# Value products of two tiles in one stretch, row sums of a head pair in one group, a third score bank

## What is computed

```
x_n = group_norm(x, 32 groups)                        # per image
qkv = einsum('bnc,oc->bno', x_n, qkv_w)               # 3 x 192 outputs
attn = softmax(einsum('bhnd,bhmd->bhnm', q, k) * 32 ** -0.5)
out = einsum('bhnm,bhmd->bhnd', attn, v)              # heads side by side: 192 channels
y = x + einsum('bnc,oc->bno', out, proj_w) + proj_b
```

## Time and profile before

| | |
|---|---|
| median of 3 runs | 1676.67 us |
| the profiled execution | 1676.28 us, its span 1674.5 us, granted clock 0.982 |
| TensorE busy | 1556.8 us (93%) |
| GpSimd busy | 1321.8 us (79%) |
| ScalarE busy | 1232.9 us (74%) |
| VectorE busy | 1188.9 us (71%) |
| value products | 3072 records, 409.8 us busy |
| row-sum products | 1152 records, 154.3 us busy |

### The profile page before, as it was taken

The page is one execution under the profiler, slowest core; times in us unless marked ns, Lnnn a source line. Parts: engine busy times, 40 slices in busy tenths (PEclk is TensorE's granted clock), DMA queues, the critical chain, the costliest instruction groups (busy, mean ns, idle before and its releaser), DMA issues.

```text
span 1674.5 us, 24581 instructions
## 1 busy us (share of the span) xinstructions
PE 1556.8 (93%) x8800; PEld 488.0 (29%) x8800; DVE 1188.9 (71%) x2022; ACT 1232.9 (74%) x2001; POOL 1321.8 (79%) x645
## 2 busy tenths in 40 slices
PE   3389999999999999999999999999999999999982
PEld 1123233232323333232332323232332323233220
DVE  3387878777787877777787777778787777777710
ACT  2138787887869787886968788796978778686770
POOL 3019888888978888888888888897888888788891
PEclk9979999999999999999999999999999999999995
DMA  2304042341515134152504325151513414141112
GB/s 71 57 26 83 15 88 47 75 86 52 103 38 103 27 85 76 52 108 52 95 25 94 57 68 93 52 103 38 98 34 77 83 52 83 52 71 33 46 34 68
DMA packets 86106, 108.87 MB, mean 65 GB/s; under 512 B 38240, under 2 KB 50912, under 8 KB 85984
## 3 DMA queue, kind: packets, MB, share of 16 engines
q1 hardware_dynamic: 85984, 107.30, 30.8%
HBM read 42.98 MB, written 13.15 MB: 34 GB/s over the span
## 4 chain that ended last, share of the span: by engine, by line
PE 80%; ACT 10%; issue 2%; DMA 1%; DVE 1%; SPq 0%; POOL 0%; POOLq 0%; ACTq 0%; DVEq 0%
PE heads_ps L550 21%; PE scores_ps L535 19%; PE max_ps L469 19%; PE sums_ps L567 7%; ACT probs L690 6%; PE extra_ps L518 2%; PE extra_ps L522 2%; PE extra_ps L519 2%; PE extra_ps L520 2%; PE extra_ps L523 2%; ACT heads_sb L653 1%; ACT xhat_b L642 1%; ACT x_res L620 1%; DMA inv_sb<-inv_rows 1%; PE extra_ps L498 0%
## 5 line engine op out<-in xcount | busy, mean ns | idle before, releaser
L844 DVE TENSOR_REDUCE half_max<-max_ps 128x1 f32<-128x512 f32 x1536 | 1005.2, 685 | 336.0 <-PE max_ps L469 321.8
L690 ACT ACTIVATE probs<-scores_ps,exp_scale 128x512 f32<-128x512 f32 x1536 | 994.1, 689 | 310.4 <-PE scores_ps L535 304.5
L743 POOL TENSOR_TENSOR prob_pairs<-probs 128x1024 f32<-128x1024 f32 x384 | 898.6, 2361 | 205.1 <-ACT probs L690 204.2
L469 PE MATMUL max_ps<-k_stack,q_stack 96*128 96x512 f16 x1536 | 593.5, 388 | 22.5 <-DVE half_max L844 13.5
L535 PE MATMUL scores_ps<-q_stack,k_stack 98*128 98x512 f16 x1536 | 586.4, 383 | 24.4 <-ACT probs L690 18.2
L550 PE MATMUL heads_ps<-probs,v_sb 128*32 128x512 f32 x3072 | 409.8, 606 | 0.1
L469 PEld LDWEIGHTS max_ps<-k_stack,q_stack 96*128 96x128 f16 x1536 | 149.7, 98 | 555.5 <-issue 429.6
L749 POOL TENSOR_TENSOR prob_pairs<-prob_pairs 128x1024 f32<-128x1024 f32 x96 | 224.3, 2358 | 0.0
L535 PEld LDWEIGHTS scores_ps<-q_stack,k_stack 98*128 98x128 f16 x1536 | 149.5, 98 | 237.3 <-ACT probs L690 171.3
L567 PE MATMUL sums_ps<-prob_pairs,ones 128*32 128x512 f32 x1152 | 154.3, 608 | 3.2 <-POOL prob_pairs L743 3.2
L550 PEld LDWEIGHTS heads_ps<-probs,v_sb 128*32 128x32 f32 x3072 | 60.5, 108 | 131.7 <-issue 129.9
(11 more groups left out here) (82 smaller groups left out, 940.0 us busy)
## 6 DMA issues: line engine op xcount, KB each, us to landing
q_stack<-qk_hi SPq DMA_DIRECT2D x96, 128.0 KB, 4.2
k_stack<-qk_hi SPq DMA_DIRECT2D x96, 128.0 KB, 5.6
inv_sb<-inv_rows SPq DMA_DIRECT2D x48, 256.0 KB
x_res<-x SPq DMA_DIRECT2D x16, 768.0 KB, 5.5
out<-x_res SPq DMA_DIRECT2D x16, 768.0 KB, 4.6
x_sb<-x SPq DMA_DIRECT2D x16, 512.0 KB, 7.4
x_sb<-x SPq DMA_DIRECT2D x32, 256.0 KB, 8.7
q_stack<-qk_lo SPq DMA_DIRECT2D x48, 128.0 KB, 4.1
```

The source lines that it names most:

```text
L469: pe.matmul(max_ps[:, bank, :], q_stack[0:STACK, par, h, P * tile:P * (tile + 1)], k_stack[0:STACK, par, h, HALF * half:HALF * (half + 1)] ...
L690: nc.scalar.activation(probs[:, a, s % RING, HALF * half:HALF * (half + 1)], scores_ps[:, u_bank(s, u), :], ACT.Exp, scale=exp_scale[:, 0: ...
L743: nc.gpsimd.tensor_tensor(prob_pairs[:, a, q, :], probs[:, a, (s - 1) % RING, :], probs[:, a, s % RING, :], ALU.add).then_inc(pairs_added, 1)
L844: nc.vector.tensor_reduce(half_max[:, a, tile, half:half + 1], max_ps[:, bank, :], AX_X, ALU.max).then_inc(max_read[bank], 1)
```

## The change

The value products of two tiles stand together, in even slots, after unit 2 (`VALUES_UNIT`); odd slots have none. The three row-sum quads of a head pair are one small product of the kind `sums`, in slots 10, 18 and 2, in `extra_ps`: twelve products in a row, right behind the value products of the slot. ScalarE copies them at the start of the next slot (`take`), and `copy_sums` and the semaphores `sums_done` and `sums_taken` go. The bank `sums_ps` becomes a third score bank. The head copy comes after unit 3 instead of 2. The later steps of the sums' way come one slot earlier (`SUMS_SPREAD` to `DIVIDED`), the moves of head pairs 1 and 2 to attn (`MOVED`) one slot earlier too, and three small products change places: qk 16 to 15, projection 17 and 18 to 16 and 17.

```
-SCORE_BANKS = 2
+SCORE_BANKS = 3
...
-QK_SLOTS = (12, 16, 19)
+QK_SLOTS = (12, 15, 19)
-PROJ_SLOTS = (17, 18, 20, 22)
+PROJ_SLOTS = (16, 17, 20, 22)
+SUMS_SLOTS = {10: 0, 18: 1, 2: 2}
...
-SUMS_TAKEN = TILES + 4
-SUMS_SPREAD = TILES + 5
-INVERTED = TILES + 6
-INV_SPREAD = TILES + 7
-INV_GATHERED = TILES + 8
-DIVIDED = TILES + 11
-MOVED = (23, 22, 22)
+SUMS_SPREAD = TILES + 4
+INVERTED = TILES + 5
+INV_SPREAD = TILES + 6
+INV_GATHERED = TILES + 7
+DIVIDED = TILES + 10
+MOVED = (23, 21, 21)
-COUNT_UNIT, HEADS_UNIT, SUMS_UNIT = 3, 2, 3
+VALUES_UNIT, HEADS_UNIT = 2, 3
...
     (TensorE, fill)
+                elif kind == "sums" and part == 0:
+                    pe.wait_ge(pairs_added, READY[-1] * (PAIRS * st.summed(i) + i + 1))
+                    for q in range(QUAD_AT, PAIRS_A_HEAD):
+                        for half in range(HALVES):
+                            for a in range(2):
+                                at = D * (2 * half + a)
+                                last = pe.matmul(extra_ps[at:at + D, :], ones[:, 0:D],
+                                                 prob_pairs[:, a, q, HALF * half:HALF * (half + 1)],
+                                                 start=(q == QUAD_AT), stop=(q == PAIRS_A_HEAD - 1))
...
     (TensorE, step)
-                        if u == 1:
-                            if s == 0 and st.tail:
-                                weigh(st.b - 1, 1 - st.parity, SLOTS - 1)
-                            elif s > 0 and st.attend:
-                                weigh(st.b, st.parity, s - 1)
+                        if u == VALUES_UNIT and s % PAIR == 0:
+                            for tile in range(s - PAIR, s):
+                                if s == 0 and st.tail:
+                                    weigh(st.b - 1, 1 - st.parity, SLOTS + tile)
+                                elif s > 0 and st.attend:
+                                    weigh(st.b, st.parity, tile)
                         if u >= 2 and st.extra(s) is not None:
                             fill(st, s, u - 2)
-                        if u == COUNT_UNIT:
-                            for j, par, q in st.due(s, PAIR_COUNTED, PAIR):
-                                count(j, q)
...
     (ScalarE, take)
+                elif kind == "sums":
+                    k = PAIRS * st.summed(i) + i
+                    if due(k):
+                        act.wait_ge(sums_spread_out, MOVE * k)
+                    nc.scalar.copy(sums_sb[:, :], extra_ps[:, :]).then_inc(extra_freed, 1)
...
     (GpSimd, pair add)
-                            if a == 0 and q >= QUAD_AT and due(k):
-                                pool.wait_ge(sums_done, COUNTED[-1] * (k - 1) + COUNTED[q])
+                            if a == 0 and q == QUAD_AT and due(k):
+                                pool.wait_ge(extra_filled, st.ordinal(s - 1) + 1)
```

More of the change, by code:

```diff
@@ L71 @@
 V_SLOTS = (7, 8, 11, 14)
-QK_SLOTS = (12, 16, 19)
+QK_SLOTS = (12, 15, 19)
 QK_LATE_SLOTS = (3, 4, 6)
-PROJ_SLOTS = (17, 18, 20, 22)
-EXTRA_SLOTS = (*SHIFT_SLOTS, *V_SLOTS, *QK_SLOTS, *QK_LATE_SLOTS, *PROJ_SLOTS)
+PROJ_SLOTS = (16, 17, 20, 22)
+SUMS_SLOTS = {10: 0, 18: 1, 2: 2}
+EXTRA_SLOTS = (*SHIFT_SLOTS, *V_SLOTS, *QK_SLOTS, *QK_LATE_SLOTS, *PROJ_SLOTS, *SUMS_SLOTS)
 assert len(set(EXTRA_SLOTS)) == len(EXTRA_SLOTS)
@@ L82 @@
 PAIR = 2
-PAIR_COUNTED = PAIR + 3
 PAIRS_A_HEAD = TILES // PAIR
@@ L90 @@
 READY = (2, 6, 8, 10)
-COUNTED = (0, 1, 2, 3)
 HEADS_TAKEN = TILES
-SUMS_TAKEN = TILES + 4
-SUMS_SPREAD = TILES + 5
-INVERTED = TILES + 6
-INV_SPREAD = TILES + 7
-INV_GATHERED = TILES + 8
-DIVIDED = TILES + 11
-MOVED = (23, 22, 22)
-COUNT_UNIT, HEADS_UNIT, SUMS_UNIT = 3, 2, 3
+SUMS_SPREAD = TILES + 4
[5 more added lines that the diff above has]
+VALUES_UNIT, HEADS_UNIT = 2, 3
 STATS = 4
@@ L143, in extra @@
             return "proj", PROJ_SLOTS.index(s)
+        if s in SUMS_SLOTS and (self.tail if SUMS_SLOTS[s] == PAIRS - 1 else self.attend):
+            return "sums", SUMS_SLOTS[s]
         return None
@@ L154, in shifted, with summed @@
         return (self.b + 1, 1 - self.parity) if pair == 0 else (self.b, self.parity)
+    def summed(self, pair):
+        return self.b - 1 if pair == PAIRS - 1 else self.b
     def made(self, i):
@@ L214, in group_norm_attention @@
         heads_ps = psum("heads_ps", [P, HALF])
-        sums_ps = psum("sums_ps", [P, HALF])
         q_stack = sb("q_stack", [P, 2, HEADS, N], F16)
@@ L306, in group_norm_attention @@
         heads_done = sem("heads_done")
-        sums_done = sem("sums_done")
         heads_taken = sem("heads_taken")
-        sums_taken = sem("sums_taken")
         sums_spread_out = sem("sums_spread_out")
@@ L398, in step @@
                         k = PAIRS * j + p
-                        sp.wait_ge(sums_taken, k + 1)
+                        sp.wait_ge(extra_freed, st.ordinal(s - 2) + 1)
                         sp.dma_start(sums_spread[:, :], sums_sb[0:P:D, :]
@@ L554, in weigh @@
                 last.then_inc(heads_done, 1)
[L556 to L570, removed]
             pe.wait_ge(setup, SETUP)
@@ L600, in take @@
                 kind, i = s > 0 and st.extra(s - 1) or (None, 0)
-                if kind in ("qk", "v"):
+                if kind in ("qk", "v", "sums"):
                     g = st.ordinal(s - 1)
@@ L653, in copy_heads @@
                     nc.scalar.copy(heads_sb[:, (par + p) % 2, :], heads_ps[:, :]).then_inc(heads_taken, 1)
-            def copy_sums(st, s):
-                for j, par, p in st.due(s, SUMS_TAKEN, TILES):
-                    k = PAIRS * j + p
-                    act.wait_ge(sums_done, COUNTED[-1] * (k + 1))
-                    if due(k):
-                        act.wait_ge(sums_spread_out, MOVE * k)
-                    nc.scalar.copy(sums_sb[:, :], sums_ps[:, :]).then_inc(sums_taken, 1)
             def between(st, s, u):
@@ L671, in between @@
                     copy_heads(st, s)
-                if u == SUMS_UNIT:
-                    copy_sums(st, s)
                 if st.tail and (s, u) in BIAS_AT:
```

## The result

The changed kernel takes 1704.04 us (median of 4 runs, 1703.77 to 1704.85) against 1676.43 us of the kernel before beside it (4 runs, 1675.66 to 1676.68): ratio 1.0166, 95% interval 1.0149 to 1.0184. It is 27.6 us slower. The profiled execution took 1704.04 us with a span of 1702.3 us, to set beside 1676.28 and 1674.5.

What follows compares the result with a forecast made beforehand. Each slot was taken to end by TensorE's work or a 3.28 us loop through ScalarE; 24.9 for middle batches, 1.3 first, 0 last, 0.8 end made +27.0 on 1676.28, median 0.4 above: 1704 us, range 1673 to 1728.

Steps and rivals of the forecast that it cites:

- case A: Whole kernel: the doubled stretch starves VectorE and ScalarE, 1704 us, own range 1687 to 1722; chance 0.67.
- middle: 14 middle batches, each 1.78 us slower (97.45 against 95.67 us): 24.9 us in all.
- the end: After GpSimd's last add three row-sum quads run instead of one, putting the copy 0.8 us later.
- The loops: Each pair of slots takes the longest way through TensorE, ScalarE or VectorE; sum 97.45 us a batch.
- The first batch: It has no projection and no sums in slot 2: 1.3 us slower.
- The last batch: It has few max products and few copies: change taken as 0.
- Rival D: Shift rows arrive 2 us late in slot 16 behind heads_lo, once a batch: 1734 us; chance 0.08.
- The small bank: Row sums share extra_ps; the reads that free it come first in all slots but 7.
- B: VectorE keeps up, a bank coming free sooner than 0.74 us: 2.3 us less a batch, 1644 us; chance 0.13.
- T and S: TensorE's (T) and ScalarE's (S) ways through a pair of slots; without VectorE's way they sum to 93.4 us a batch.
- C: TensorE binds throughout and all 4.6 us a batch come out: 1607 us; chance 0.06.
- E: Gains of nine pairs and losses of three cancel: 1673 to 1680 us; chance 0.06.

Runs made afterwards that it cites:

- the half-width maxima: VectorE's maxima over 256 of 512 columns: 1646.23 us on the changed kernel with shift rows first, 1608.36 us on that with single value products.

## Why the prediction was right, step by step

The forecast was case A at 1704 us, the measurement 1704.04. The mechanism is the one that was named, and it is there in the size that the pairs of slots give. That the number is exact is luck: start and middle were put 14 us too high and the end 15 us too low. With the shift rows first, where no score waits for them, the kernel takes 1690.9 us, 15 more than before and not 27, near the lower end of the range that A was given (1687).

**The loops held.** Pair by pair in the steady state, measured from the first max product behind the stretch and its small product to the same place two slots on (medians of ten batches), in us, counted values in brackets: from slot 10, 7.54 (7.54); 12, 7.24 (7.32); 14, 7.62 (7.62); 16, 10.40 (10.48); 18, 7.56 (7.54); 20, 7.56 (7.57); 22, 6.88 (6.92); 0, 8.94 (9.02); 2, 7.54 (7.54); 4, 7.48 (7.56); 6, 8.24 (8.25); 8, 10.01 (10.09). No pair is off by more than 0.08. From slot 0 to 8, 8 to 16 and 16 to 0 the head copies stand 32.2, 32.4 and 32.4 us apart (32.4, 32.6, 32.5).

**The middle was over-counted, 24.9 us for 14 batches where 13 measured periods lost 14.2.** The difference per batch is 1.07, not 1.78: the count was 0.4 us long for the change and 0.3 short for the kernel before. For the change it is 0.08 long in each of five pairs. For the kernel before nearly all of it is one pair, from slot 10, 8.35 us and not 8.07, where ScalarE also adds the bias. Two small errors of opposite sign in two sums of 96 us make a third of the answer. I had said that the count was short for before; set against the measured 95.94 instead of 95.67, it gives 1.51 a batch.

**The first batch** was put at +1.3; up to slot 8 of the second it gained 1.8.

**The last batch was put at 0 and the end at +0.8; together with batch 14 they lost 15.4.** This is the step that failed: the moves ahead of the shift rows were to cost 0. Rival D, shift rows late behind `heads_lo`, which had a chance of 0.08 for one wait a batch, is true of the last batches and all but absent in between (waits of 0.55 us at 751.26 and 0.15 at 1042.59). The work for images ahead ends there: slots 8 to 16 of batch 14 have two q and k products fewer, and slots 0 to 8 of batch 15 have of the small products only the row sums and the transpose (25 records instead of 50); the max products are still all there at the first two waits and halved before the third. So TensorE comes to the first score sooner, while GpSimd's four adds and `heads_lo` take as long as ever: the second piece of the shift rows goes out 28.87, 28.88 and 28.89 us after the first score of slot 0 in batches 13, 14 and 15, while the first score of slot 8 starts at 32.09 and 31.44 in batches 13 and 14 and could have started at 27.91 in batch 15. The margin that I computed in the middle, 28.85 - 28.4, does not exist there, and I did not compute it again. The run with the shift rows first shows 13.7 us for it.

**The small bank.** "The reads that free it come first in all slots but 7" was wrong: besides 0.94 us in slot 7, TensorE waits 0.29 us in slots 5 and 13 for VectorE's residual of qk, and 0.67 and 0.35 us in slots 17 and 21 for its read of the projection. The pairs agree with the count without these waits, so they cost little here; with the statistics moved, the one in slot 17 did.

**Rivals.** B, VectorE keeps up: excluded by the half-width maxima. They take VectorE's loop away and give 44.6 us; the count had T and S alone at 93.4 us a batch, 94.1 with the pair from slot 6 left as it is, and 94.4 was measured. C, all of the drained time comes out: excluded. The entries and exits did go (quads 0.87 apart in the doubled stretch, 1.74 from 825.16 to 826.90), as the Trainium skill, TensorEngine Tiling, Key Properties, says of a change of tiling mode; but that gives 4.6 us a batch to an engine that then waits. E, gains and losses cancel: excluded, the three pairs with row sums lose 5.0 us a batch and the nine others together gain 3.9 (counted 5.2 and 3.4).

**What the forecast did not see** is that the change contains a faster kernel: everything but the doubling, 1619.9 us with the shift rows first. Its gain over the kernel before must come from the third bank or from the new places of the products, since the group of row sums alone costs 8.5 us; no run has single products after unit 2 with two banks, so the third bank's own share is not shown. The prediction weighed the change as a whole and said of the third bank only that it was inside S.

## What to carry to other kernels

Before joining stretches of work that feed nobody, compare their length with what the filled banks keep the readers busy: here three banks of 0.585 us for ScalarE and three of 0.597 for VectorE, against 1.9 and 4.5 us. A saving on the engine that looks like the bound is worth what it is only as long as its readers don't run dry. Try an added bank without the longer stretches first: here it saved 161 us under them, and the fastest kernel still was the one that had the bank and not the stretches. Compute the margin of a reordered DMA again in the first and the last rounds, where the rest of the loop is shorter, and set a difference of two counted sums against the measured one wherever there is one.

## What the runs showed of the hardware

- A separate stretch of four fp32 products of 32 rows takes 1.10 us of TensorE, each further one directly behind it 0.87: joining saves 0.22 to 0.23 us.
- Doubling the stretches costs 71 us with three score banks and the row sums in one group (1690.87 against 1619.88), and 65 us with two banks and the row sums apart (1740.76 against 1675.70). The whole change costs 27.6 us with three banks and 190 us with two, at equal work.
- The granted clock near the end differs between versions that differ only in the order of some DMAs: 0.87 from 1590 to 1650 us in the changed kernel, 0.94 from 1582 to 1642 us with the shift rows first, and the last twelve products took 5.35 us in the one and 2.78 in the other.
